# A vision transformer tower on one core: output products of the second attention moved between the halves of the value products

## The reference

```python
qkv = x @ W_qkv + b_qkv                                  # 8 heads of 16
dots = einsum('bhid,bhjd->bhij', q, k) * dk ** (-0.5)
dots = dots * mask                                       # causal, masked scores are 0, not -inf
attn = softmax(dots, axis=-1)
out_attn = einsum('bhij,bhjd->bhid', attn, v) ... @ W_out + b_out
# x_cema: an exponential moving average over the images, 16 states per feature
y = w[0] * out_attn + w[1] * x_cema
h = layernorm(h + y)
# next: gates = h @ gate_w (8 experts), sinkhorn, top-k, expert products
```

## Time and profile before

| | |
|---|---|
| median of 3 runs | 859.21 us (856.6 to 860.98) |
| the profiled execution | 858.74 us, its span 857.0 us |
| mean granted TensorE clock | 0.818 |
| TensorE busy | 647.8 us, 76% |
| VectorE | 503.9 us, 59% |
| ScalarE | 348.4 us, 41% |
| GpSimd | 230.8 us, 27% |
| DMA | mean 65 GB/s |

### The profile page before, as it was taken

How to read it: one execution, slowest core, us unless ns; L and a number is a source line. 1 busy time by engine, 2 the same in 40 slices (tenths; PEclk the granted TensorE clock), 3 DMA queues, 4 the chain that set the end, 5 groups by cost and what they waited for, 6 DMA issues and landing times. The chain is left out here.

```text
span 857.0 us, 21432 instructions
## 1 busy us (share of the span) xinstructions
PE 647.8 (76%) x8455; PEld 525.0 (61%) x8455; DVE 503.9 (59%) x904; ACT 348.4 (41%) x871; POOL 230.8 (27%) x270
## 2 busy tenths in 40 slices
PE   2999999999999986730987778668688888982002
PEld 2788888888888865610942466358577777772001
DVE  0375666666666665254212687768677667764862
ACT  0113444444444444210632333432366676666600
POOL 1363333333334440000011233310334443330001
PEclk9999999999999997655579977955698888885555
DMA  8533333333333000027900620000000000001200
GB/s 345 192 147 114 115 114 125 124 128 147 129 132 114 1 2 2 2 98 157 142 8 0 73 29 0 0 1 0 2 2 2 0 0 0 3 2 44 70 12 4
DMA packets 28658, 55.35 MB, mean 65 GB/s; under 512 B 12274, under 2 KB 25698, under 8 KB 26114
## 3 DMA queue, kind: packets, MB, share of 16 engines
q1 hardware_dynamic: 28515, 54.62, 21.4%
q0 software_dynamic: 96, 0.07, 0.0%
HBM read 48.14 MB, written 6.55 MB: 64 GB/s over the span
## 5 line engine op out<-in xcount | busy, mean ns | idle before, releaser
L375 PE MATMUL a_bank<-a_x,a_tok_w 128*128 128x256 f32 (+1 forms) x608 | 150.3, 390 | 15.8 <-DVE a_ht L555 15.8
L375 PEld LDWEIGHTS a_bank<-a_x,a_tok_w 128*128 128x128 f32 (+1 forms) x608 | 113.1, 192 | 37.1 <-DMA tables<-in_tables 15.8
L124 POOL TENSOR_TENSOR a_qt<-a_qp,data 128x512 f32<-128x512 f32 x64 | 71.8, 1153 | 2.1 <-POOL a_qp L617 1.6
L617 POOL TENSOR_TENSOR a_qp<-a_rope 128x260 f32<-128x260 f32 x16 | 11.7, 734 | 175.4 <-DVE a_rope L499 175.4
L1376 ACT ACTIVATE b_at<-b_bank 65x512 f32<-65x512 f32 x64 | 34.8, 601 | 42.8 <-PE b_bank L1223 42.8
L282 ACT ACTIVATE a_at<-a_bank 65x256 f32<-65x256 f32 x128 | 38.8, 389 | 25.9 <-PE a_bank L259 25.9
L493 DVE SCALAR_TENSOR_TENSOR a_ht<-a_bank,data 128x256 f32<-128x256 f32 x16 | 7.7, 483 | 64.3 <-PE a_bank L375 64.3
L1460 POOL TENSOR_TENSOR b_e<-b_e,b_inv 128x585 f32<-128x585 f32 (+1 forms) x32 | 35.5, 1108 | 20.1 <-DVE b_inv L1311 19.8
L259 PE MATMUL a_bank<-a_mix,a_e 64*65 64x64 f32 x1024 | 40.6, 234 | 0.0
L259 PEld LDWEIGHTS a_bank<-a_mix,a_e 64*65 64x65 f32 x1024 | 36.1, 147 | 4.0 <-issue 3.4
L195 ACT ACTIVATE a_e<-a_e 128x390 f32<-128x390 f32 (+1 forms) x48 | 24.3, 510 | 33.2 <-DVE a_e L175 33.2
(11 more groups left out here) (252 smaller groups left out, 1521.5 us busy)
## 6 DMA issues: line engine op xcount, KB each, us to landing
a_x<-in_x SPq DMA_DIRECT2D x16, 2304.0 KB, 7.8
lag_rows<-r_kernel SPq DMA_DIRECT2D x1, 4192.5 KB, 39.2
lags<-lag_rows SPq DMA_DIRECT2D x1, 2112.5 KB
base<-places SPq DMA_DIRECT2D x1, 2080.0 KB
out<-e_plain SPq DMA_DIRECT2D x16, 130.0 KB
expert_weights<-in_w SPq DMA_DIRECT2D x2, 1024.0 KB, 5.8
a_tok_w<-in_tok_w SPq DMA_DIRECT2D x1, 1152.0 KB, 6.7
data<-in_data SPq DMA_DIRECT2D x1, 910.5 KB, 4.8
```

The lines of the kernel that those rows point to most:

```text
L124: nc.gpsimd.tensor_tensor(qt[:, b * BLOCKS * P:(b + 1) * BLOCKS * P].rearrange("p (c h i) -> p c h i", i=qb, h=HEADS), wide(by_image[:, b, ...
L375: mm = nc.tensor.matmul(banks[0][:, 0:GP], w[0:rows, k * DIM:(k + 1) * DIM], x[p][0:rows, k * GP:(k + 1) * GP], start=(k == 0), stop=(k == ...
```

## The change

On TensorE, `output(g - 1)` moves from behind `scores(g + 1)` to between the two halves of the value products of `g`. `turn_rows` and `gates` work one step later (`g - 2` in place of `g - 1`): `turn_rows` behind `scores(g + 1)`, `gates` behind `turn_last`. The loop has one step more. `turn_rows` gets a wait on `gates_saved`, `turn_last` one on `ot_ready`. On ScalarE, `save_rows(g - 2)` opens the step, `save_gates(g - 2)` follows the second `save_pair`, and `queries_keys(g + 2)` comes ahead of the first `exponent`. VectorE's and GpSimd's code is as it was.

```diff
@@ turn_rows @@
                 pe.wait_ge(S.z_ready, g + 1)
+
+                wait_past(pe, S.gates_saved, g)
@@ TensorE @@
-            for g, i, p in pipeline(pe, 2, GROUPS + 1):
+            for g, i, p in pipeline(pe, 2, GROUPS + 2):
                 if exists(g + 1):
                     scores(g + 1)
-                if exists(g - 1):
-                    output(g - 1)
+                if exists(g - 2):
+                    turn_rows(g - 2)
                 if exists(g):
                     pe.wait_ge(S.probs_ready, 2 * g + 1)
 
                     wait_past(pe, S.at_ready, 5 * g)
                     turn_pair(g, p, 0)
+
+                    wait_past(pe, S.ot_ready, g)
                     turn_last(g, p)
+                if exists(g - 2):
+                    gates(g - 2)
...
                     values_of_image(nc, 0, at, vs[p], obank)
                     values_of_image(nc, 1, at, vs[p], obank)
                 if exists(g - 1):
-                    turn_rows(g - 1)
+                    output(g - 1)
                 if exists(g):
                     pe.wait_ge(S.at_ready, 5 * g + 5)
                     values_of_image(nc, 2, at, vs[p], obank)
                     values_of_image(nc, 3, at, vs[p], obank).then_inc(S.av_done, 1)
-                if exists(g - 1):
-                    gates(g - 1)
@@ ScalarE @@
             for g, i, p in pipeline(act, 2, GROUPS + 2):
+                if exists(g - 2):
+                    save_rows(g - 2)
                 if exists(g):
                     save_pair(g, 0)
                     save_last(g)
+                if exists(g + 2):
+                    queries_keys(g + 2)
                 if exists(g + 1):
                     exponent(g + 1, 0, e[1 - p])
-                if exists(g + 2):
-                    queries_keys(g + 2)
                 if exists(g):
                     save_pair(g, 1)
+                if exists(g - 2):
+                    save_gates(g - 2)
                 if exists(g + 1):
                     save_values(g + 1, 1 - p)
                     exponent(g + 1, 1, e[1 - p])
                 if exists(g - 1):
-                    save_rows(g - 1)
                     average(g - 1)
                 if exists(g):
                     save_heads(nc, act, g, obank, ot, S)
-                if exists(g - 1):
-                    save_gates(g - 1)
                 if exists(g - 2):
                     squares(g - 2)
```

## The result

| | before | after |
|---|---|---|
| median | 859.6 us (856.6 to 860.98, 4 runs) | 901.49 us (898.71 to 904.17, 4 runs) |
| ratio | | 1.0492, 95% interval 1.0449 to 1.0535 |
| span of the profiled execution | 857.0 us | 901.8 us |
| mean granted TensorE clock | 0.818 | 0.799 |

The kernel became slower by 4.9%; 880 us were forecast, 867 to 896 the range.

What follows compares the result with a forecast made beforehand. TensorE was taken to set the 10.12 us lap before; afterwards a cross-engine ring of 10.16 us plus 1.14 for the clock gives 11.30. 858.74 + 15.3 (13 laps) + 6.4 (end) = 880.4, forecast 880 us, range 867 to 896.

Steps and rivals of the forecast that it cites:

- The wait before `output`: TensorE, between the value halves: waits about 0.65 us for the saved gates, in place of the earlier 0.42 us.
- the one before the first turning pair: TensorE, start of its turning work: a new wait of about 1.6 us per lap for GpSimd's `normalise`.
- VectorE standing still before `residual`: VectorE's in-order queue: idle 2 to 4 us in every lap until the late `output` is done.
- no wait is left before `gates`: TensorE: the 0.61 us wait for ScalarE's saved turned rows goes.
- the ring: Loop through TensorE, ScalarE, VectorE and GpSimd from one first turning pair to the next, claimed to set the lap.
- The clock: TensorE's drop to 1.2 GHz, expected to stay once a lap and cost 1.14 us, for a lap of 11.30 us.
- the sum: Addition of the forecast's terms: lap 10.16 + 1.14 = 11.30 us; 858.74 + 15.3 + 6.4 = 880.4 us in all.
- two drops: Rival: both TensorE waits are each followed by 1.2 GHz; 888 to 896 us, middle 892; chance 0.18.
- The ring at full clock: The loop between successive first turning pairs with TensorE at 2.4 GHz: 10.16 us, against 8.98 before.
- The ends: End of the stage: +3.0 us between the last first turning pairs, +3.4 to the last `output`, 0 after it.
- `queries_keys` ahead of `exponent`: ScalarE's order: exponentials 1.4 us later, keys as much earlier, both inside slack; cost nothing.
- The rival of the full clock: Rival: TensorE stays at 2.4 GHz, lap 10.16 us, only the stage's end is longer; 863 us; chance 0.10.

Runs made afterwards that it cites:

- experiment 1: Changed kernel with VectorE doing `residual` and `total_of_rows` between the two `invert`s instead of ahead of both: 851.66 us, ratio 0.9921 to the kernel before.
- experiment 5: Changed kernel with `save_gates` ahead of the second `save_pair` on ScalarE: 888.83 us, ratio 1.0346 to the kernel before.
- experiment 7: One extra VectorE reduction of constants (0.68 us) between `total_of_rows` and the first `invert`: changed kernel 911.21 us, kernel before 858.66 us.
- experiment 10: Kernel of experiment 2 with GpSimd's copy of `h` right behind `last_queries` instead of last in its step: 866.14 us, ratio 1.0066 to the kernel before.
- experiment 2: Changed kernel with five extra unread products in TensorE's wait before the first turning pair: 875.43 us, ratio 1.0180 to the kernel before.
- experiment 9: Changed kernel with `gates` behind the values instead of ahead of the queries and keys: 895.99 us, ratio 1.0426 to the kernel before.
- experiment 4: Kernel before with three extra unread products, one before the second value half and two ahead of `gates`: 845.56 us, ratio 0.9836.

## Why the prediction was wrong

**The direction and the mechanism held.** The wait before `output` for gates saved behind the copies was forecast at 0.65 us and is 0.75 in most laps; the one before the first turning pair at 1.6 and is 1.4 to 2.0; VectorE standing still before `residual` was to be seen, and is (5.5 us, where I had said 2 to 4 for a shorter lap); no wait is left before `gates`. Experiments 1, 5 and 7 each change one term of the ring, and the time follows; the 50 us of experiment 1 are the ring and the clock together.

What was mis-sized:

- **The clock**, taken at 1.14 us a lap; this is the step that failed. "Its price when all that it slows lies on the path is today's 1.14 us" carried over a stretch of 3.4 us that lies in the scores and `output`. In the changed kernel the stretch lasts about 6.8 us in most laps and lies mostly in the turning, `gates`, queries, keys and values, all of them on the ring: from the first turning pair to the end of the second 6.72 us where the sum has 4.07 and experiment 10, at full clock, 3.95. Per lap that is 2.85 us (13.08 against 10.23), two and a half times the term; 2.16 come back when the clock is kept (experiment 2), since the wait for the copy then appears. The rival "two drops" had 2.3 us as its upper bound, which the range just took in (896); the drop is one of double length, and dearer than that bound. Why it is so long stays open (experiment 9).
- **The ring at full clock**, 10.16 us, was right for what it held: 10.19 in experiment 10. It was not the whole of the lap at full clock, which is 10.92, since I had followed it along the engines that released each other in the trace of before; a queue that had slack there (GpSimd, busy 3.81 of 10.10 us) was not followed past the instruction that I needed, through `centre`, the second `normalise` and the copy to the values. In the changed kernel this cost nothing in the twelve laps, because the work at 1.2 GHz ahead of the values is longer. The sum needed 13.08 against 11.30 in each of twelve laps, 21.4 us in all, and nearly all of that is the clock's.
- **The ends.** The end of the stage was summed at +6.4 and is +9.5. The last two first turning pairs lie 12.15 us apart (+4.7, summed +3.0), from the second turning pair to the last `output` it is 8.21 us (+4.5, summed +3.4), and what follows takes 0.9 more (summed 0), with the last two `output`s at 1.2 GHz (1.94 us each, where 1.1 was summed); 0.6 less lies in between. `queries_keys` ahead of `exponent` was put at "nothing"; it costs 0.7 us in the first lap, where ScalarE has no slack yet (the values' save comes later, and the scores wait 1.60 us for it, against 0.89), and nothing in the steady laps, where I had looked. The other 1.0 us of the first two laps is not shown to be its work. Against that the third lap, which the prediction counted as a full one of 11.30, took 7.49 us: `turn_rows` and `gates` are not yet in it, and no wait stands before `output` or the turning pair.

The profiled execution took 904.17 us, 23.8 above the sum of 880.4: 21.4 in the twelve laps, -3.8 in the third, +1.7 in the first two, +3.1 at the end (9.5 against 6.4), and 1.0 ahead of the stage, 23.4 in all.

The rival of the full clock was not the case of this kernel, but experiments 2 and 10 show its value: 875 us, and 866 with the copy out of the way, where 863 was said. The rule of the Trainium skill (TensorE: Matmul & The Clock Gate, "HAM oscillation — how this bites in real kernels"), which asks only for no long idle gaps, is contradicted here in two kernels: before the change waits of 0.42 and 0.61 us bring the drop, and filled they don't (experiment 4); after it waits of 0.33 to 0.75 and 1.4 to 2.0 us do. It fits a third, experiment 1, whose waits of 0.76 and 0.23 to 0.76 us a lap leave the clock at 1.00.

## What to carry to other kernels

When an operation is moved later on one engine, look at who reads its result and what is queued behind that reader: here VectorE's `residual` held back inverts that had nothing to do with it, and moving two calls behind one turned +42 us into -7. Write the new order as a ring and add up its terms on every engine's queue to the end of the step, not only along today's releasers. Where TensorE waits a microsecond or two in each turn, price the clock apart; a few idle products in the wait both measure it and get it back (14 us in the kernel before, 26 in the changed one). What comes back can be less than the clock costs, when a wait that the slow work had covered then shows (here 0.7 us a lap).

## What was not expected of the hardware

- TensorE kept the clock at 1.00 with waits of 0.76 and 0.23 to 0.76 us in each lap of 9.25 us (experiment 1), and lost it with 0.42 and 0.61 us in a lap of 8.98 (the kernel before). How long it stands still does not alone decide.
- Once fallen, the clock stayed at 0.50 for about 6.8 us in most laps of the changed kernel, with TensorE busy for all of 6.50 us of it; before the change it came back after 3.4 us in the laps, and after 6.9 us once, at the end of the stage (8.00 us from 766 at a mean of 0.57). In experiment 9 there were stretches of 3.25 to 3.5 and of 10.25 to 10.5 us.
- What 1.2 GHz costs depends on the work: 64 score products take 1.29 us against 0.91, the value products of a group 1.91 against 1.04.
- GpSimd's copy of 128 x 260 elements takes 0.39 us before the change (0.393 mean) and 0.87 after it (0.866), and VectorE's 128 x 520 subtraction 0.70 before and up to 1.18 after, when it meets an operation of GpSimd. In the rows of experiment 10 the times fit turns taken: the second `normalise` ends at 698.62, and the subtraction, though it starts at 698.09, ends only at 699.18, about its own 0.70 after some 698.5; the copy starts at 698.57 and ends at 699.43, about its own 0.39 after some 699.05. The Trainium skill (SBUF — State Buffer, "SBUF: two separate sides") says that GpSimd and a VectorE operation with two inputs in SBUF take one pair of ports in turns, each for a whole instruction; the trace agrees, with these numbers. No run here takes one of the two operations away.
